# Pass over the weights in pairs of tiles through single buffers, and the square roots one GELU group earlier

## Chip, cores and metric

The kernel runs on all 8 cores of one Trainium2 chip, the same program on each with its own rows. The metric is the device time of the slowest core, in microseconds (us).

## What is computed

The input x is 4 x 8192 x 1024 in float32. It goes through a state-space layer and a quantised feed-forward layer, each behind a layer norm and added to its input:

```python
# attn: u = LN(x) @ W_in.T ; h_t = h_{t-1}*Abar + u_t*Bbar ; y = (h*C) @ W_out.T
x = x + attn(layernorm(x))
def _quant_weight(w):                       # ternary weights, one scale for the whole matrix
    s = clip(mean(abs(w)), 1e-5, None)
    return clip(round(w / s), -1, 1) * s
def _quant_act(x):                          # 8-bit activations, one scale per token
    scale = 127.0 / clip(max(abs(x), axis=-1, keepdims=True), 1e-5, None)
    return clip(round(x * scale), -128, 127) / scale
# w1: 4096 x 1024, w2: 1024 x 4096
h = gelu(quant_act(layernorm(x)) @ quant_weight(w1).T)
x = x + quant_act(h) @ quant_weight(w2).T
```

The scale of a weight matrix needs the mean of all its absolute values. So each core reads both matrices twice: pass 1 sums absolute values, pass 2 rounds to ternary and keeps the result in SBUF.

## The kernel before

Each core makes 4096 tokens of output. A program has four stages, with semaphores written out by hand on five engines.

**Set-up.** Small parameters, W_in and W_out are loaded, cast and transposed. `woctB0` and `winB` are parts of the bf16 buffer `k2`.

**Pass 1** (VectorE L427 to L446, `for j in range(NWT)`). The 64 tiles of 128 x 1024 float32 (512 KB each; 32 of w1, 32 of w2) come over three rings: tile t on ring t % 3, ring 0 issued by ScalarE, ring 1 by SyncE, ring 2 by GpSimd. Each ring has two buffers (`WSTG`) and at most one transfer in the air: `w_dma` (L151 to L162) waits until the ring's transfer before has landed, and, through `wa`, until VectorE has reduced the tile two places back in the ring. VectorE takes the tiles in order, one `tensor_reduce` each (L430). After the last one it makes the second scale (L447 to L459) with TensorE's help.

**Pass 2** (L463 to L475). The same 64 tiles over the same rings; VectorE does three operations on a tile (L470, L472, L474), TensorE transposes it (L694), ScalarE copies it to `t1T` or `t2T` (L264, L267). The first tiles of pass 2 may be fetched as soon as the ring's next-to-last tiles of pass 1 are reduced. On ScalarE the transfer of tile j stands in the same loop as the copies.

**Main loop.** Blocks of 128 tokens, 64 in all; the first 32 (NCH) run only the recurrence, so that the state is right at the second half, and the last 32 do everything. The engines run skewed: in pass b, VectorE works on the norms of blocks b+1 and b+2 and then on the maximum and rounding of block b-NCH-1, for which TensorE makes the first product (mm1) in the same pass.
TensorE's order in a pass is: `te_fa` (transposes L753, small product L763), `te_mm1` in 8 groups of 32 matmuls (L733) into two PSUM banks in turn, with the out-projection and a transpose behind group 0, then the first half of the second product `te_mm2` (32 matmuls, L789), then `te_btr` (L771, L774, L777: brings the per-token scale across partitions), then the second half of `te_mm2`. Group g of mm1 waits until GELU g-2 has emptied its bank.
ScalarE's order is: copy `xnfm` (L324), cast `hb_s`, GELUs 0 to 5 (L303), `se_sqrt2(b+1)` (L310), `se_sqrt1(b+2)` (L316), GELUs 6 and 7, copy `k1fm` (L292), `se_rowbc` (L330, L333). `sqrt2` needs VectorE's L527, `sqrt1` needs its L544, which comes later.
VectorE's order is: L592, scan L489, output L499, `ve_fb1a` (L509, L511, L514), `ve_fb1b` (L521 to L527), `ve_fa1a` (L533), `ve_fa1b` (L539 to L544), `ve_fb2` (L563 to L585, waits for `sqrt2`), `ve_fa2` (L552 to L556, waits for `sqrt1`), then `ve_back_a`: the maximum over the hidden layer (L599, waits for GELU 7), the scale (L603 to L611), and rounding in four quarters (L622, L623).

Of the kernel before, what the change touches and what calls it, by code (L numbers as in the profile page):

```python
# [6 lines left out]
F32 = mybir.dt.float32  # L7
BF16 = mybir.dt.bfloat16
AF = mybir.ActivationFunctionType
ALU = mybir.AluOpType  # L10
AX = mybir.AxisListType
# [9 lines left out]
W1_TILES = 32  # L21
W2_TILES = 32
NWT = W1_TILES + W2_TILES
# [6 lines left out]
        _PT_ORDER.append(("k", _b - NCH))  # L30
PT_IDX = {key: i for i, key in enumerate(_PT_ORDER)}

W_SLOT = []
_rc = [0, 0, 0]
for _t in range(2 * NWT):
    _r = (_t % NWT) % 3
    W_SLOT.append((_r, _rc[_r]))
    _rc[_r] += 1
W_RING = [[t for t in range(2 * NWT) if W_SLOT[t][0] == r] for r in range(3)]


def build_nc():
    nc = bass.Bass("TRN2", target_bir_lowering=False)
    dr = {}
    for n, shp in [("xh", (TOK, D)), ("xo", (TOK, D)),
# [22 lines left out]
    h_sb = sbt("h_sb", (128, H))  # L68
    vs2 = sbt("vs2", (128, 2048))
    x2 = x2_3 + [vs2[:, 1024:2048]]  # L70
    k2 = sbt("k2", (128, H), BF16)
# [19 lines left out]
    TL = {n: TLblk[:, i:i + 1] for i, n in enumerate(TLn)}  # L91
# [17 lines left out]
    wstB = [h_sb[:, 1024:2048], h_sb[:, 2048:3072]]  # L109
    wstC = [h_sb[:, 3072:4096], out_s0[:, 0:1024]]  # L110
    WSTG = [wst, wstB, wstC]
    wqb = [k2[:, 0:1024], k2[:, 1024:2048]]
    winB = k2[:, 2048:3072]
    woctB0 = k2[:, 3072:4096]
# [2 lines left out]
    wmul = x2_3[0]  # L117
    wrnd = x2_3[1]
    wabs = hred
# [8 lines left out]
    t2T_qv = t2T.rearrange("p (q f r) -> p q f r", q=4, f=8)  # L128
    pT_v8 = pT.rearrange("p (k t) -> p k t", k=8)

    SEMS = ["lx", "lw", "lws", "lwg", "lp", "lo", "gp", "prep",
            "wa", "s1b", "s2b", "q1", "q1T", "q1e",
            "zoh1", "zoh2", "k1m", "k1me", "winc", "winTd", "winTe",
            "wotc", "wotTd", "wotTe", "woctr", "wcT1", "wcT2", "sc1m", "sc2m",
# [5 lines left out]
    with ExitStack() as ctx:  # L140
# [7 lines left out]
        def wtile(j):  # L148
            return w1_v[j] if j < W1_TILES else \
                w2_v[(j - W1_TILES) // 4, (j - W1_TILES) % 4]  # L150

        def w_dma(eng, r, t):
            _, si = W_SLOT[t]
            if si >= 2:
                tp = W_RING[r][si - 2]
                if tp < NWT:
                    eng.wait_ge(S["wa"], tp + 1)
                else:
                    eng.wait_ge(S["q1"], tp - NWT + 1)
            eng.wait_ge(S[WSEM[r]], 16 * si)  # L160
            eng.dma_start(out=WSTG[r][si % 2],
                          in_=wtile(t % NWT)).then_inc(S[WSEM[r]], 16)  # L162

        @block.sync
        def _(sync):
            for di, nm in enumerate(["logA", "Bp", "Cp", "logdt", "gate", "win"]):
                dst = {"logA": P64["logA"], "Bp": P64["Bp"], "Cp": P64["Cp"],
                       "logdt": sc11, "gate": gt11}.get(nm)
                d = winF[0:64, :] if nm == "win" else dst[:]
                sync.wait_ge(S["lp"], 16 * di)  # L170
                sync.dma_start(out=d, in_=dr[nm][:, :]).then_inc(S["lp"], 16)
            wo_v = dr["wout"].rearrange("(a p) n -> a p n", p=128)
            for a in range(8):
                sync.wait_ge(S["lo"], 16 * a)
                sync.dma_start(out=wost[:, a * 64:(a + 1) * 64],
                               in_=wo_v[a]).then_inc(S["lo"], 16)
            for t in W_RING[1]:
                w_dma(sync, 1, t)
            for it in range(NIT):
                sync.wait_ge(S["lx"], 16 * it)  # L180
                if it >= 2:
                    sync.wait_ge(S["xn_"], it - 1)
                    sync.wait_ge(S["sq1a"], it - 1)
                    if it - 2 >= NCH:
                        sync.wait_ge(S["x2_"], it - 2 - NCH + 1)
                    else:
                        sync.wait_ge(S["scan"], it - 1)
                src = dr["xh"] if it < NCH else dr["xo"]
                c = it if it < NCH else it - NCH
                sync.dma_start(out=xb[it % 2][:],  # L190
                               in_=src[c * 128:(c + 1) * 128, :]).then_inc(S["lx"], 16)

        @block.gpsimd
        def _(g):
            g.iota(identD[:], pattern=[[-1, 128]], base=0, channel_multiplier=1,
                   allow_small_or_imprecise_dtypes=True)
            g.drain().then_inc(S["gp"], 1)
            for t in W_RING[2]:
                w_dma(g, 2, t)
            def gp_sq2(it):  # L200
                oi = it - NCH
                g.wait_ge(S["x2_"], oi + 1)
                if it >= NCH + 1:
                    g.wait_ge(S["k1s_"], it - NCH)
                g.tensor_tensor(scr_sq[:], x2[oi % 4][:], x2[oi % 4][:],  # L205
                                ALU.mult)
                g.drain().then_inc(S["sq2a"], 1)

            def gp_sq1(it):
                g.wait_ge(S["lx"], 16 * (it + 1))  # L210
                if it >= 1:
                    g.wait_ge(S["r1d"], it)
                if it - NCH >= 1:
                    g.wait_ge(S["r2d"], it - NCH)
                g.tensor_tensor(scr_sq[:], xb[it % 2][:], xb[it % 2][:],  # L215
                                ALU.mult)
                g.drain().then_inc(S["sq1a"], 1)

            gp_sq1(0)
            gp_sq1(1)  # L220
            for b in range(NIT + 3):
                oi3 = b - NCH - 3
                if NCH <= b + 1 < NIT:
                    gp_sq2(b + 1)
                if b + 2 < NIT:
                    gp_sq1(b + 2)
                if 0 <= oi3 < NCH:
                    g.wait_ge(S["od"], 16 * oi3)
                    g.wait_ge(S["outv"], oi3 + 1)
                    g.dma_start(out=dr["out"][oi3 * 128:(oi3 + 1) * 128, :],  # L230
                                in_=out_s[oi3 % 2][:]).then_inc(S["od"], 16)
            g.wait_ge(S["od"], 16 * NCH)

        @block.scalar
        def _(s):
# [14 lines left out]
            s.wait_ge(S["wotTd"], 1)  # L250
            s.copy(woctB0[0:64, :], pT[0:64, 0:1024])
            s.drain().then_inc(S["wotTe"], 1)
            for t in W_RING[0]:
                if t < NWT:
                    w_dma(s, 0, t)
            s.wait_ge(S["sc1m"], 2)
            s.copy(TL["r1b"][:], pmisc[:, 2:3])
            s.copy(TL["s1o"][:], pmisc[:, 3:4])
# [80 lines left out]
            for b in range(NIT + 2):  # L339
                oi1 = b - NCH - 1  # L340
                has1 = 0 <= oi1 < NCH
                if b + 1 < NIT:
                    se_xnfm(b + 1)
                if NCH <= b + 1 < NIT:
                    se_hb(b + 1)
                if has1:
                    for g in range(0, 6):
                        se_gelu(oi1, g)
                if NCH <= b + 1 < NIT:
                    se_sqrt2(b + 1)  # L350
                if b + 2 < NIT:
                    se_sqrt1(b + 2)
                if has1:
                    se_gelu(oi1, 6)
                    se_gelu(oi1, 7)
                if 0 <= b - NCH < NCH:
                    se_k1fm(b - NCH)
                if has1:
                    se_rowbc(oi1)

        @block.vector
        def _(v):
# [61 lines left out]
            v.tensor_single_scalar(woct[0:64, :], woctB0[0:64, :],  # L424
                                   P64["Cp"][:, 0:1], ALU.mult)
            D_().then_inc(S["woctr"], 1)
            for j in range(NWT):  # L427
                _r, _si = W_SLOT[j]
                v.wait_ge(S[WSEM[_r]], 16 * (_si + 1))
                v.tensor_reduce(wabs[:, j:j + 1], WSTG[_r][_si % 2], AX.X, ALU.add,  # L430
                                apply_absolute_value=True)
                D_().then_inc(S["wa"], 1)
                if j == W1_TILES - 1:
                    v.tensor_reduce(TL["wcol"][:, 0:1], wabs[:, 0:W1_TILES],
                                    AX.X, ALU.add)
                    D_().then_inc(S["wcT1"], 1)
                    v.wait_ge(S["wcT1"], 2)
                    v.tensor_reduce(wtot[0:1, 0:1], pmisc[0:1, 128:256], AX.X,
                                    ALU.add); D_()
                    v.tensor_scalar(pack[0:1, 2:3], wtot[0:1, 0:1],  # L440
                                    1.0 / (H * D), 1e-5, op0=ALU.mult,
                                    op1=ALU.max); D_()
                    v.reciprocal(pack[0:1, 0:1], pack[0:1, 2:3]); D_()
                    v.tensor_scalar(pack[0:1, 1:2], pack[0:1, 2:3],
                                    1.0 / 127.0, None, op0=ALU.mult)
                    D_().then_inc(S["sc1m"], 1)  # L446
            v.wait_ge(S["s1b"], 1)  # L447
            v.tensor_reduce(TL["wcol"][:, 0:1], wabs[:, W1_TILES:NWT],
                            AX.X, ALU.add)
            D_().then_inc(S["wcT2"], 1)  # L450
            v.wait_ge(S["wcT2"], 2)
# [10 lines left out]
            for j in range(NWT):  # L462
                rb = TL["r1b"] if j < W1_TILES else TL["r2b"]  # L463
                if j == W1_TILES:
                    v.wait_ge(S["s2b"], 1)
                _r, _si = W_SLOT[NWT + j]
                v.wait_ge(S[WSEM[_r]], 16 * (_si + 1))
                if j >= 2:
                    v.wait_ge(S["q1T"], j - 1)
                v.tensor_single_scalar(wmul[:], WSTG[_r][_si % 2], rb[:, 0:1],  # L470
                                       ALU.mult); D_()
                v.tensor_scalar(wrnd[:], wmul[:], TL["C_t"][:, 0:1],  # L472
                                TL["nC_t"][:, 0:1], op0=ALU.add, op1=ALU.add); D_()
# [376 lines left out]
```

## Time and profile before

| | us |
|---|---|
| median of the runs | 2277.48 |
| lowest and highest of 2 runs | 2272.14, 2282.82 |
| the profiled execution | 2280.37 |
| its span, slowest core (core 2) | 2278.8 |
| spans of the 8 cores | 2260.1 to 2278.8 |

The span runs from the first to the last instruction of the slowest core; the execution's own time is 1.6 us more. All shares and rows are of core 2. A line L12 is line 12 of the kernel before. DVE is VectorE, ACT ScalarE, PE TensorE, POOL GpSimd, SP SyncE. "Idle before" is the time an engine stood still ahead of an instruction, with what ended it.

### The profile page before, as it was taken

How to read it: one execution, taken by the hardware profiler on the slowest of the kernel's cores; microseconds unless marked ns; L12 is line 12 of the kernel's file. 1: busy time of each engine (PE TensorE's matmuls, PEld its weight loads, DVE VectorE, ACT ScalarE, POOL GpSimd, SP SyncE). 2: the span in 40 equal slices, each digit the busy share in tenths (PEclk: the TensorE clock that was granted, in tenths of full speed). 3: DMA queues.
4: the chain of work that ended last, by engine and by line, in shares of the span. 5: the costliest groups of instructions: out<-in, count | busy, mean ns of one | idle time of the engine just before them, and what ended most of it. 6: DMA issues, size and time to landing. Idle time of an engine off the chain costs nothing.

```text
span 2278.8 us, 34173 instructions; the slowest of 8 cores (2260.1 to 2278.8 us)
## 1 busy us (share of the span) xinstructions
PE 1225.5 (54%) x12248; PEld 852.5 (37%) x12248; DVE 1485.8 (65%) x2187; ACT 444.0 (19%) x682; POOL 223.1 (10%) x175
## 2 busy tenths in 40 slices
PE   0002222211111126777867776786778678777887
PEld 0001111111111115445644554564455456445554
DVE  3565555555555557777777777777777777777653
ACT  0002222211110112212321221222122122212210
POOL 0000000011111111000100100010010001001000
PEclk9999999999999997979988998998899889889989
DMA  4874344111111100000100000010000001000000
GB/s 138 251 247 140 118 138 157 41 42 47 46 46 46 46 19 20 19 20 20 38 19 20 29 29 19 20 38 20 19 29 29 19 19 39 20 19 20 19 11 28
DMA packets 33900, 120.18 MB, mean 53 GB/s; under 512 B 4996, under 2 KB 4996, under 8 KB 33732
## 3 DMA queue, kind: packets, MB, share of 16 engines
q1 hardware_dynamic: 16740, 56.11, 7.6%
q0 software_dynamic: 10656, 38.80, 4.5%
q10 hardware_dynamic: 6336, 23.07, 3.4%
q8 instruction: 100, 1.64, 0.3%
q14 instruction: 68, 0.56, 0.1%
HBM read 101.19 MB, written 16.78 MB: 52 GB/s over the span
## 4 chain that ended last, share of the span: by engine, by line
PE 37%; DVE 34%; DMA 10%; issue 8%; ACT 7%; DVEq 2%; ACTq 1%; POOLq 0%; SPq 0%; POOL 0%
PE pout L789 13%; DVE hred L599 10%; PE pm1b L733 8%; PE pm1a L733 8%; DMA vs<-w 5%; ACT xnfm L324 3%; DMA h_sb<-w 2%; PE pmisc L763 2%; DVE xn L556 2%; PE pT L753 2%; DVE TLblk L553 2%; DVE TLblk L539 2%; DMA out_s<-w 2%; DVE vs L533 2%; DVE TLblk L572 2%
## 5 line engine op out<-in xcount | busy, mean ns | idle before, releaser
L789 PE MATMUL pout<-t2T,k 128*128 128x512 bf16 x2048 | 507.7, 411 | 4.1 <-DVEq L504 4.1
L789 PEld LDWEIGHTS pout<-t2T,k 128*128 128x128 bf16 x2048 | 210.1, 105 | 279.6 <-issue 84.4
L733 PE MATMUL pm1a<-k1fm,t1T 128*128 128x128 bf16 x4096 | 253.7, 221 | 0.0
L733 PE MATMUL pm1b<-k1fm,t1T 128*128 128x128 bf16 x4096 | 251.3, 220 | 0.0
L622 DVE TENSOR_TENSOR vs<-h_sb,sc2bc 128x1024 f32<-128x1024 f32 x128 | 156.8, 1225 | 134.9 <-ACTq L334 75.2
L599 DVE TENSOR_REDUCE hred<-h_sb 128x128 f32<-128x4096 f32 x32 | 224.1, 7004 | 28.6 <-ACTq L305 22.8
L733 PEld LDWEIGHTS pm1a<-k1fm,t1T 128*128 128x128 bf16 x4096 | 236.7, 99 | 3.4 <-issue 0.3
L733 PEld LDWEIGHTS pm1b<-k1fm,t1T 128*128 128x128 bf16 x4096 | 235.7, 98 | 0.0
L753 PE MATMUL pT<-identb,xn 128*128 128x128 bf16 x512 | 53.5, 268 | 295.2 <-DVEq L558 295.2
L694 PE MATMUL pT<-identb,k 128*128 128x128 bf16 x512 | 64.7, 306 | 190.5 <-DVEq L476 190.5
L753 PEld LDWEIGHTS pT<-identb,xn 128*128 128x128 bf16 x512 | 42.7, 120 | 310.1 <-issue 303.5
L215 POOL TENSOR_TENSOR xn<-xb 128x1024 f32<-128x1024 f32 x64 | 121.1, 1892 | 379.9 <-DMA xb<-xh 291.4
L324 ACT COPY xnfm<-pT 128x1024 bf16<-128x1024 bf16 x64 | 64.8, 1012 | 402.9 <-PE pT L753 402.7
L771 PE MATMUL pmisc<-ident,hred 128*128 128x128 f32 x32 | 14.0, 437 | 219.2 <-DVEq L601 219.2
L205 POOL TENSOR_TENSOR xn<-x 128x1024 f32<-128x1024 f32 x24 | 45.2, 1884 | 858.7 <-DVEq L513 858.7
L694 PEld LDWEIGHTS pT<-identb,k 128*128 128x128 bf16 x512 | 49.5, 137 | 205.5 <-issue 205.5
L592 DVE TENSOR_SCALAR u_s<-pmisc,P64blk 64x128 f32<-64x128 f32 x64 | 21.9, 343 | 145.6 <-PE pmisc L763 145.3
L623 DVE TENSOR_SCALAR k<-vs,TLblk 128x1024 bf16<-128x1024 f32 x128 | 104.0, 813 | 10.8 <-issue 0.9
L763 PE MATMUL pmisc<-xnfm,winT 128*64 128x128 bf16 x512 | 54.2, 270 | 98.0 <-ACTq L325 98.0
L303 ACT ACTIVATE h_sb<-pm1b 128x512 f32<-128x512 f32 x128 | 76.4, 597 | 154.4 <-PE pm1b L733 149.8
L303 ACT ACTIVATE h_sb<-pm1a 128x512 f32<-128x512 f32 x128 | 76.4, 597 | 115.9 <-PE pm1a L733 93.0
L771 PEld LDWEIGHTS pmisc<-ident,hred 128*128 128x128 f32 x32 | 5.8, 180 | 233.8 <-issue 233.8
(152 smaller groups left out, 1444.7 us busy)
## 6 DMA issues: line engine op xcount, KB each, us to landing
vs<-w ACTq DMA_DIRECT2D x44, 512.0 KB, 4.8
h_sb<-w SPq DMA_DIRECT2D x42, 512.0 KB, 4.7
xb<-xh SPq DMA_DIRECT2D x32, 512.0 KB, 3.4
xb<-xo SPq DMA_DIRECT2D x32, 512.0 KB, 3.5
out<-out_s POOLq DMA_DIRECT2D x32, 512.0 KB, 3.0
h_sb<-w POOLq DMA_DIRECT2D x21, 512.0 KB, 5.3
out_s<-w POOLq DMA_DIRECT2D x21, 512.0 KB, 4.9
xn<-win SPq DMA_DIRECT2D x1, 256.0 KB
```

The costliest lines, as they stand in the source:

```text
L215: g.tensor_tensor(scr_sq[:], xb[it % 2][:], xb[it % 2][:], ALU.mult)
L303: s.activation(h_sb[:, g * 512:(g + 1) * 512], bank[:], AF.Gelu, bias=0.0, scale=1.0)
L324: s.copy(xnfm[it % 2][:], pT[:])
L533: v.tensor_scalar(vs2[:, 0:1024], xb[it % 2][:], 0.0, None, op0=ALU.add, op1=ALU.add, accum_out=TL["sm"][:, 0:1]); D_()
L599: v.tensor_reduce(hred[:, 0:128], h3, AX.X, ALU.max, apply_absolute_value=True)
L622: v.tensor_tensor(vq, hs, bcb, ALU.mult); D_()
L623: v.tensor_scalar(k2[:, q * 1024:(q + 1) * 1024], vs2[:, 0:1024], TL["C_t"][:, 0:1], TL["nC_t"][:, 0:1], op0=ALU.add, op1=ALU.add); D_()
L694: ti = t.transpose(pT[:, f * 128:(f + 1) * 128], wqb[j % 2][:, f * 128:(f + 1) * 128], identb[:])
L733: ti = t.matmul(reg, t1T[:, k * 4096 + m * 128:k * 4096 + (m + 1) * 128], k1fm[oi % 2][:, k * 128:(k + 1) * 128], start=(k == 0), stop=(k ...
L753: ti = t.transpose(pT[:, f * 128:(f + 1) * 128], xn[:, f * 128:(f + 1) * 128], identb[:])
L763: ti = t.matmul(pmisc[0:64, 0:128], winT[:, k * 64:(k + 1) * 64], xnfm[it % 2][:, k * 128:(k + 1) * 128], start=(k == 0), stop=(k == 7))
L789: ti = t.matmul(pout[:, d * 512:(d + 1) * 512], k2[:, hk * 128:(hk + 1) * 128], t2T[:, hk * 1024 + d * 512:hk * 1024 + d * 512 + 512], sta ...
```

## The change

It has two parts.

1. In pass 1 two neighbouring tiles are one pair: 32 pairs of 1 MB, each loaded by one DMA (a 128 x 2 x 1024 pattern for w1, 2048 neighbouring columns for w2) and reduced by one `tensor_reduce` over 2048 columns. Each ring has one buffer of 2048 columns in place of two of 1024 (`WPAIR`), so a ring's next transfer waits until its last pair is reduced. Ring 2's buffer is the whole of `k2`, so its first transfer waits for `woctr`. Pass 2 has the tiles, rings and buffers it had, but the first two transfers of every ring wait until the whole of pass 1 is reduced.
2. In the main loop ScalarE does GELUs 0 to 4, then the two square roots, then GELUs 5 to 7.

```diff
+P1_RING = [[p for p in range(NP1) if p % 3 == r] for r in range(3)]
...
+    k2f = k2.bitcast(F32)
+    WPAIR = [vs2[:, 0:2048], h_sb[:, 1024:3072], k2f[:, 0:2048]]
...
+        def w_dma1(eng, r, i):
+            p = P1_RING[r][i]
+            if i >= 1:
+                pprev = P1_RING[r][i - 1]
+                eng.wait_ge(S["wa"], pprev + 1)
+            if r == 2 and i == 0:
+                eng.wait_ge(S["woctr"], 1)
+            eng.wait_ge(S[WSEM[r]], 16 * i)
+            eng.dma_start(out=WPAIR[r].rearrange("p (c d) -> p c d", c=2),
+                          in_=wpairsrc(p)).then_inc(S[WSEM[r]], 16)
...
         def w_dma(eng, r, t):
-            if si >= 2:
-                tp = W_RING[r][si - 2]
-                if tp < NWT:
-                    eng.wait_ge(S["wa"], tp + 1)
-                else:
-                    eng.wait_ge(S["q1"], tp - NWT + 1)
+            if i2 < 2:
+                eng.wait_ge(S["wa"], NP1)
+            else:
+                tp = P2_RING[r][i2 - 2]
+                eng.wait_ge(S["q1"], tp + 1)
...
                 if has1:
-                    for g in range(0, 6):
+                    for g in range(0, 5):
                         se_gelu(oi1, g)
                 if NCH <= b + 1 < NIT:
                     se_sqrt2(b + 1)
                 if b + 2 < NIT:
                     se_sqrt1(b + 2)
                 if has1:
-                    se_gelu(oi1, 6)
-                    se_gelu(oi1, 7)
+                    for g in range(5, 8):
+                        se_gelu(oi1, g)
...
-            for j in range(NWT):
-                _r, _si = W_SLOT[j]
+            for p in range(NP1):
+                _r, _si = P1_SLOT[p]
                 v.wait_ge(S[WSEM[_r]], 16 * (_si + 1))
-                v.tensor_reduce(wabs[:, j:j + 1], WSTG[_r][_si % 2], AX.X, ALU.add,
+                v.tensor_reduce(wabs[:, p:p + 1], WPAIR[_r], AX.X, ALU.add,
                                 apply_absolute_value=True)
```

## Rows read from the trace of the kernel before

**Rows 1.** Busy time of the engines in three stages, and each stage's granted clock.

```profile
core 2: us, PE busy (x) PEld busy (x) DVE busy (x) ACT busy (x) POOL busy (x), PEclk, DMA share, GB/s
34.00:166.00 132.00, 0.93 (x3) 0.57 (x3) 79.17 (x71) 0.22 (x2) 10.55 (x20) 1.00 0.82 253
166.00:422.00 256.00, 64.65 (x507) 49.32 (x507) 145.15 (x197) 63.98 (x65) 12.64 (x21) 1.00 0.39 130
...
885.00:2210.00 1325.00, 1007.93 (x10452) 694.50 (x10451) 971.78 (x1367) 313.19 (x503) 124.79 (x86) 0.88 0.07 23
```

**Rows 2.** Waits from 38 to 158 us: waiter, releaser, us in total, times, longest.

```profile
POOL out_s L161 <- DMA h_sb<-w: 51.1, 8, 7.3
POOL h_sb L161 <- DMA out_s<-w: 42.5, 8, 5.8
SPq L157 <- DVEq L432: 104.4, 20, 8.6
```

**Rows 3.** Median time from issue to landing, whole page, section on DMA issues.

```profile
vs<-w ACTq DMA_DIRECT2D x44, 512.0 KB, 4.8
xb<-xh SPq DMA_DIRECT2D x32, 512.0 KB, 3.4
```

**Rows 4.** Timeline of pass 1 and its end: start, duration, instruction, [idle before].

```profile
33.66 36.62 ACTq L161 DMA_DIRECT2D vs<-w  x8
...
45.64 1.22 DVE L430 TENSOR_REDUCE hred<-out_s 128x1 f32<-128x1024 f32 x1 [0.19 <-issue]
...
164.52 1.22 DVE L430 TENSOR_REDUCE hred<-vs 128x1 f32<-128x1024 f32 x1 [0.19 <-issue]
...
168.05 0.75 DVE L470 TENSOR_SCALAR x<-vs,TLblk 128x1024 f32<-128x1024 f32 x1 [0.33 <-issue]
...
169.77 0.69 DVE L474 TENSOR_SCALAR k<-x 128x1024 bf16<-128x1024 f32 x1
```

**Rows 5.** Timeline of one pass of the main loop, around the square roots.

```profile
1534.58 1.28 ACT L310 ACT_TABLE_LOAD   x1
1535.37 1.95 PE L733 MATMUL pm1b<-k1fm,t1T 128*128 128x128 bf16 x32
1535.38 0.15 DVE L544 TENSOR_SCALAR TLblk<-TLblk 128x1 f32<-128x1 f32 x1
1535.87 0.20 ACT L310 ACTIVATE TLblk<-TLblk 128x1 f32<-128x1 f32 x1
1536.20 0.16 DVE L563 RECIPROCAL TLblk<-TLblk 128x1 f32<-128x1 f32 x1 [0.67 <-ACTq L312]
...
1537.16 7.07 PE L789 MATMUL pout<-t2T,k 128*128 128x512 bf16 x32
1537.87 0.60 ACT L303 ACTIVATE h_sb<-pm1a 128x512 f32<-128x512 f32 x1
...
1543.89 6.99 DVE L599 TENSOR_REDUCE hred<-h_sb 128x128 f32<-128x4096 f32 x1 [0.19 <-issue]
1551.17 0.45 PE L771 MATMUL pmisc<-ident,hred 128*128 128x128 f32 x1 [6.95 <-DVEq L601]
...
1554.78 8.78 PE L789 MATMUL pout<-t2T,k 128*128 128x512 bf16 x32
```

**Rows 6.** The line L563 over the whole span: idle of VectorE before it.

```profile
  ACTq L312: 26.9, 30
```

**Rows 7.** TensorE alone in short stretches: busy time (matmuls), granted clock, DMA.

```profile
1019.75:1025.77 6.02, 6.02 (x16) 0.50 0.00 0
1025.77:1028.50 2.73, 2.73 (x14) 1.00 0.00 0
1065.68:1070.15 4.47, 4.47 (x12) 0.50 0.00 0
1244.07:1247.64 3.57, 3.57 (x10) 0.50 0.00 0
1288.44:1292.01 3.57, 3.57 (x10) 0.50 0.00 0
1510.47:1513.88 3.41, 3.41 (x10) 0.50 0.00 0
1548.00:1554.78 6.78, 1.51 (x4) 0.50 0.00 0
1554.78:1558.25 3.47, 3.47 (x10) 0.50 0.00 0
1558.25:1563.55 5.30, 5.30 (x28) 1.00 0.00 0
```

More of the change, by code:

```diff
@@ L31 @@
 PT_IDX = {key: i for i, key in enumerate(_PT_ORDER)}
[L33 to L39, printed above, removed]
+NP1 = NWT // 2
+P1_RING = [[p for p in range(NP1) if p % 3 == r] for r in range(3)]
+P1_SLOT = {}
+for _r in range(3):
+    for _i, _p in enumerate(P1_RING[_r]):
+        P1_SLOT[_p] = (_r, _i)
+P2_RING = [[j for j in range(NWT) if j % 3 == r] for r in range(3)]
+P2_SLOT = {}
+for _r in range(3):
+    for _i, _j in enumerate(P2_RING[_r]):
+        P2_SLOT[_j] = (_r, len(P1_RING[_r]) + _i)
 def build_nc():
@@ L129, in build_nc @@
     pT_v8 = pT.rearrange("p (k t) -> p k t", k=8)
-    SEMS = ["lx", "lw", "lws", "lwg", "lp", "lo", "gp", "prep",
+    SEMS = ["lx", "lw", "lws", "lwg", "lwt", "lp", "lo", "gp", "prep",
             "wa", "s1b", "s2b", "q1", "q1T", "q1e",
@@ L150, in wtile, with wpairsrc @@
                 w2_v[(j - W1_TILES) // 4, (j - W1_TILES) % 4]
-        def w_dma(eng, r, t):
-            _, si = W_SLOT[t]
-            if si >= 2:
-                tp = W_RING[r][si - 2]
-                if tp < NWT:
-                    eng.wait_ge(S["wa"], tp + 1)
-                else:
-                    eng.wait_ge(S["q1"], tp - NWT + 1)
+        w1_pv = dr["w1"].rearrange("(a c p) d -> a p c d", c=2, p=128)
+        w2_pv = dr["w2"].rearrange("(i p) (b e) -> i b p e", p=128, e=2048)
+        def wpairsrc(p):
+            if p < W1_TILES // 2:
+                return w1_pv[p]
+            pp = p - W1_TILES // 2
+            return w2_pv[pp // 2, pp % 2].rearrange("p (c d) -> p c d", c=2)
+        def w_dma1(eng, r, i):
[8 more added lines that the diff above has]
+                          in_=wpairsrc(p)).then_inc(S[WSEM[r]], 16)
+        def w_dma(eng, r, t):
+            j = t - NWT
+            _, si = P2_SLOT[j]
+            i2 = si - len(P1_RING[r])
+            if i2 < 2:
[3 more added lines that the diff above has]
+                eng.wait_ge(S["q1"], tp + 1)
             eng.wait_ge(S[WSEM[r]], 16 * si)
-            eng.dma_start(out=WSTG[r][si % 2],
-                          in_=wtile(t % NWT)).then_inc(S[WSEM[r]], 16)
+            eng.dma_start(out=WSTG[r][i2 % 2],
+                          in_=wtile(j)).then_inc(S[WSEM[r]], 16)
         @block.sync
@@ L176, in _ @@
                                in_=wo_v[a]).then_inc(S["lo"], 16)
-            for t in W_RING[1]:
-                w_dma(sync, 1, t)
+            for i in range(len(P1_RING[1])):
+                w_dma1(sync, 1, i)
+            for j in P2_RING[1]:
+                w_dma(sync, 1, NWT + j)
             for it in range(NIT):
@@ L197, in _ @@
             g.drain().then_inc(S["gp"], 1)
-            for t in W_RING[2]:
-                w_dma(g, 2, t)
+            for i in range(len(P1_RING[2])):
+                w_dma1(g, 2, i)
+            for j in P2_RING[2]:
+                w_dma(g, 2, NWT + j)
             def gp_sq2(it):
@@ L252, in _ @@
             s.drain().then_inc(S["wotTe"], 1)
-            for t in W_RING[0]:
-                if t < NWT:
-                    w_dma(s, 0, t)
+            for i in range(len(P1_RING[0])):
+                w_dma1(s, 0, i)
             s.wait_ge(S["sc1m"], 2)
@@ L426, in _ @@
             D_().then_inc(S["woctr"], 1)
-            for j in range(NWT):
-                _r, _si = W_SLOT[j]
+            for p in range(NP1):
+                _r, _si = P1_SLOT[p]
                 v.wait_ge(S[WSEM[_r]], 16 * (_si + 1))
-                v.tensor_reduce(wabs[:, j:j + 1], WSTG[_r][_si % 2], AX.X, ALU.add,
+                v.tensor_reduce(wabs[:, p:p + 1], WPAIR[_r], AX.X, ALU.add,
                                 apply_absolute_value=True)
                 D_().then_inc(S["wa"], 1)
-                if j == W1_TILES - 1:
-                    v.tensor_reduce(TL["wcol"][:, 0:1], wabs[:, 0:W1_TILES],
+                if p == NP1 // 2 - 1:
+                    v.tensor_reduce(TL["wcol"][:, 0:1], wabs[:, 0:NP1 // 2],
                                     AX.X, ALU.add)
@@ L447, in _ @@
             v.wait_ge(S["s1b"], 1)
-            v.tensor_reduce(TL["wcol"][:, 0:1], wabs[:, W1_TILES:NWT],
+            v.tensor_reduce(TL["wcol"][:, 0:1], wabs[:, NP1 // 2:NP1],
                             AX.X, ALU.add)
@@ L465, in _ @@
                     v.wait_ge(S["s2b"], 1)
-                _r, _si = W_SLOT[NWT + j]
+                _r, _si = P2_SLOT[j]
+                _i2 = _si - len(P1_RING[_r])
                 v.wait_ge(S[WSEM[_r]], 16 * (_si + 1))
@@ L469, in _ @@
                     v.wait_ge(S["q1T"], j - 1)
-                v.tensor_single_scalar(wmul[:], WSTG[_r][_si % 2], rb[:, 0:1],
+                v.tensor_single_scalar(wmul[:], WSTG[_r][_i2 % 2], rb[:, 0:1],
                                        ALU.mult); D_()
```

## The prediction

> **What bounds the kernel now.** I cut the span into stages first, because the two parts of the change live in different ones [rows 1]. Pass 1 (34 to 166 us) is 6% of the span, pass 2 11%, and the main loop with everything in it (885 to 2210 us) 58%. In pass 1 TensorE and ScalarE are idle, VectorE is busy 60%, and the DMA engines 82%: it is bound by transfers.
>
> The waits say how. GpSimd's ring waits 93.6 us in 16 waits for its own last landing, 5.85 us each [rows 2]. With its issue of some 0.55 us this ring turns every 6.4 us and never stops. SyncE's ring has time left: it waits 104.4 us for VectorE, which takes tiles in order and so goes at the pace of the slowest ring. The pace from the sixth reduce (45.64) to the 64th (164.52) is 118.9 us for 58 tiles, 2.05 each, 12.3 for six [rows 4].
>
> In the main loop no engine is full (TensorE 76%, VectorE 73%), so I followed one pass in the timeline [rows 5]. VectorE has L544 done at 1535.53 but starts L563 only at 1536.20, because ScalarE's `sqrt2` is queued behind GELU 5 and a table load of 1.28 us. Over the whole run that idle time is 26.9 us in 30 waits [rows 6], with some long ones at the start; the usual one is 0.67 or a little less. From L563 on VectorE runs without a gap to L599, then TensorE's L771, then the second half of mm2 at 1554.78, which leads to the next pass.
>
> The clock is the third thing to see [rows 7]. TensorE has done nothing since 1544.2 when the clock falls from 2.4 to 1.2 GHz at 1548.0, and it rises at 1558.25, after 3.47 us of matmuls of the second half. That half takes 8.78 us, the first 7.07 at full clock: the difference, 1.71, is half of 3.47. So a low stretch of s us under matmuls costs s/2.
>
> Now set the rises beside the starts. The second half starts at 1019.75, 1065.68, 1244.07, 1288.44, 1510.47 and 1554.78; the clock rises at 1025.77, 1070.15, 1247.64, 1292.01, 1513.88 and 1558.25. Between the first and the last rise lie 12 passes and 532.48 us, 44.373 a pass, and the neighbouring pairs give 44.38, 44.37 and 44.37. The starts don't keep this step: 45.93, 44.37, 44.31. The low stretch makes up the difference: pass length less s/2 is 45.93 - 3.01 = 42.92, 44.37 - 1.79 = 42.58, 44.31 - 1.71 = 42.60. A pass whose work is about 42.6 us is held at 44.37: if it starts its second half early, the rise doesn't come early with it, s grows, and half of what was gained is paid at once. The rest is paid in the passes behind (s: 6.02, 4.47, ... 3.57, 3.57). This is the choice on which my forecast of the loop rests.
>
> **Part 1, pass 1.** Removed: 32 of 64 transfers and reduces. The 2048-column reduce has no row; it lies between 1.22 (the cost of 1024) and 2.44 (twice that), and nearer the latter, since an instruction over one column still takes 0.15 (L544 [rows 5]): 2 x (1.22 - 0.15) + 0.15 = 2.3. VectorE then needs 32 x 2.5 = 80 us of 130, so it is no bound, but now it stands in the ring: a cycle of a ring is landing + 2.3 + about 0.2 + issue 0.55, for 1 MB. Per ring before: 12.3 us for 1 MB.
> The landing of 1 MB has no row either. At least: 5.85 and another 512 KB at the whole measured rate of 253 GB/s (2.1), so 7.9 and a cycle of 10.9; then three rings move 3.15 MB in 10.9, 289 GB/s. At most: two landings of 512 KB, 11.7, cycle 14.7. If the second 512 KB gets half the rate (4.1), it is 13.0. Fewer transfers are in the air while a ring waits for its reduce, so the others go faster; I take 12.0, between 10.9 and 13.0, which is 262 GB/s and near the measured rate. Start: ring 0 issues at 33.66 as before and the first pair lands at about 40; pairs 1 (early, on SyncE) and 2 (issued after `woctr`, at 34.2) follow, so three pairs are reduced at about 47, as six tiles are now (45.64 + 1.22). Left are 29 pairs, 9.67 cycles: 9.67 x (12.0 - 12.3) = -2.9. The last reduce is 1.1 longer.
> Hand-over to pass 2: now VectorE ends pass 1 at 165.74 and starts L470 at 168.05, 2.3 us, the tile long there. After it, all three rings wait for the last `wa`; a landing takes 4.8 on ScalarE's ring [rows 3], plus 0.1: +2.6. Queued behind these waits are only later weight transfers; ScalarE has its scale copy done by then (before `w_dma` of tile 64 in its order). Pass 2 itself is unchanged, so it is moved and not stretched. Sum of part 1: -2.9 + 1.1 + 2.6 = +0.8; bounds 9.67 x (10.9 - 12.3) + 3.7 = -10 and 9.67 x (14.7 - 12.3) + 3.7 = +27.
> The Trainium skill (DMA: Bandwidth & Descriptors, Anatomy of one DMA) fits a transfer as about 2.0 us and its bytes at 436 GB/s; by that 1 MB costs 2 us less than two of 512 KB, an estimate of 19 us less for pass 1. The landing of 5.85 us for 512 KB, where that fit has 3.2, shows that the eight cores are not in that regime. Against the change speaks the rule to double-buffer (Trainium Kernel Development and Optimization, Best Practices).
>
> **Part 2, the main loop.** `sqrt2` now stands behind GELU 4, whose input is one group (1.8 us) earlier, and is done before L544 ends. L563 then starts 0.19 behind L544, as other instructions do that wait for nothing [rows 5]: 0.67 - 0.19 = 0.48 less, say 0.45. Nothing below zero is to be had from VectorE.
> What ScalarE does later: `sqrt1` can't start before 1535.53 + 0.1; with 0.20 for itself and 1.4 for the table load GELU 5 starts at 1537.2 and ends at 1537.8, where it ended at 1534.4, just ahead of the table load. Group 7 of mm1 waits for that bank: 1537.95 in place of 1535.37, end 1539.9 (1541.9 at the low clock), GELU 7 at the latest at 1542.6. L599 starts at 1543.4, so it is covered by 0.8 to 2.8 us. The first half of mm2 ends at about 1547.0, and L771 is due at 1550.7: covered by 3.7. Queued behind are the `k1fm` copy and the row copies, not due before 1553. TensorE stands idle 2.5 us before group 7, and the clock may fall there; that is hidden as long as these covers last. The number of table loads is unchanged.
> So the work of a pass falls from 42.6 to 42.15. By the lock, s goes from 3.5 to 4.4, within the 6.02 that rows 7 show, and the pass stays at 44.37. Over the loop only the earlier phase at its end is kept, about -1.
>
> **Sum** against the profiled 2280.4: +0.8 - 1 = 2280.2; the median of the runs is 2.9 lower. I say **2277**.
>
> **Rivals.**
> A (forecast): held loop, pass 1 within 10 us: 2277, its own range 2267 to 2290. 0.62.
> B: larger transfers pay. Cycle of 10.9 or less: -10 to -20 us, 2262. For it: DMA share 0.82, not 1; against: landings of 5.85 under load. 0.12.
> C: the lock gives way. 28 passes x 0.45 = 13 us, 2264; if the low stretch under the second half vanishes also, 28 x (0.45 + 1.71) = 60 us, 2217. For it: with the first half of mm2 ending at 1547.0 and L771 at 1550.7, TensorE's idle time falls from 6.9 to about 4 us, and the clock might stay up. The Trainium skill (TensorE: Matmul & The Clock Gate, HAM oscillation) has short gaps leave the clock alone. Against the large one: TensorE also has only 1.5 us of work from 1548.0 to 1554.8, and the clock didn't rise in it. 0.14 for the small gain, 0.05 for the large.
> D, slower: one buffer a ring costs pass 1 its overlap. With landings of 1 MB at 11.7 the cycle is 14.7: +27 us, 2303; it is slower as soon as the landing exceeds 9.3. For it: 104.4 us of waits of SyncE's ring for VectorE, which now every ring has. Against: TensorE and ScalarE's idle, and freed rate. 0.05.
> E, slower by more: the clock falls in the gap before group 7 and stays low. Low for all of group 7 and the first half of mm2, they end at 1556.0, L771 is 5.3 us late, 28 x 5.3 = +148 us, 2425. It decides from a low stretch of 7.4 us on (twice the 3.7 of cover). Rows 7 show low stretches under matmuls of 3.4 to 6.0 us. 0.02.
>
> **Numbers.** A range from 2248 to 2296 leaves out the large C, E and the ends of B and D. A measurement of this kernel tells about 2% from no change. Below 2232 only the large C: 0.05. Above 2323: E, 0.02. Within: 0.93.
>
> **What would show it.** Pass 1: 32 reduces of 2.3 us ending near 166, at 250 to 270 GB/s. Hand-over of 5 us before the first L470. Main loop: idle before L563 near 0.2, a new idle time of about 2.5 us of TensorE before group 7, with a dip of the clock there; passes still 44.37 apart with s of about 4.4. Wrong if the passes are 43.9 or less apart, if L599 waits for GELU 7, or if pass 1 is more than 10 us off.

## The result, and the profile after

The changed kernel takes 2256.51 us (median of 11 runs, 2249.18 to 2264.93) against 2279.46 for the kernel before in the same comparison (10 runs). The ratio is 0.9897 with a 95% interval of 0.988 to 0.9914: 23 us, 1.0%, less. The forecast was 2277 with a range of 2248 to 2296. The profiled execution of the changed kernel has a slowest core (core 0) of 2261.1 us; the cores lie between 2238.3 and 2261.1.

Where the 23 us went is read at six marks in both traces, as the median over the eight cores, in us:

| mark | before | after | difference |
|---|---|---|---|
| last reduce of pass 1 ends | 163.6 | 145.0 | -18.6 |
| pass 2 starts | 165.9 | 150.8 | -15.1 |
| pass 2 ends | 415.9 | 398.9 | -17.0 |
| first maximum of the main loop (before L599, after L630) | 867.6 | 849.8 | -17.8 |
| last maximum | 2225.8 | 2201.6 | -24.2 |
| end of the span | 2270.7 | 2249.1 | -21.6 |

So the start of the main loop is some 18 us earlier, by pass 1, and its end with what follows gives some 4 us more. This is one execution of each kernel; how far others with the same code differ is said below. The stages of the changed kernel (stretch, busy us and count of each engine, granted clock, DMA share, GB/s), to be set against [rows 1]:

```profile
core 0: us, PE busy (x) PEld busy (x) DVE busy (x) ACT busy (x) POOL busy (x), PEclk, DMA share, GB/s
34.00:146.00 112.00, 1.30 (x4) 0.66 (x4) 74.70 (x41) 0.32 (x2) 6.08 (x10) 1.00 0.92 288
150.00:411.00 261.00, 63.73 (x504) 48.77 (x504) 144.01 (x192) 63.98 (x65) 12.98 (x21) 1.00 0.39 127
```

Pass 1 moves 288 GB/s in place of 253. The timeline of its third pair, its last pair and the first operation of pass 2:

```profile
42.21 2.29 DVE L460 TENSOR_REDUCE hred<-k 128x1 f32<-128x2048 f32 x1 [0.19 <-issue]
...
142.03 2.29 DVE L460 TENSOR_REDUCE hred<-h_sb 128x1 f32<-128x2048 f32 x1 [0.57 <-DMA h_sb<-w]
...
149.58 0.75 DVE L501 TENSOR_SCALAR x<-vs,TLblk 128x1024 f32<-128x1024 f32 x1 [2.91 <-DMA vs<-w]
```

A reduce over 2048 columns takes 2.29, as estimated. From the third pair (end 44.50) to the 32nd (144.32) are 99.8 us for 29 pairs, 10.3 for three, where six tiles took 12.3 [rows 4]. The hand-over takes 5.3 us, and in the last 2.91 of it VectorE has nothing left to wait for but the landing. Landings in the middle of the pass:

```profile
k<-w POOLq DMA_DIRECT2D x9, 1024.0 KB, 7.4
vs<-w ACTq DMA_DIRECT2D x9, 1024.0 KB, 8.1
```

and who waited for whom from 42 to 138 us (compare [rows 2]): GpSimd's ring no longer runs from landing to landing, it waits for the reduce of its pair.

```profile
POOL k L175 <- DVEq L462: 88.9, 9, 11.4
```

One pass of the main loop of the changed kernel, lines as in [rows 5]:

```profile
1515.06 1.28 ACT L340 ACT_TABLE_LOAD   x1
...
1516.35 0.20 ACT L340 ACTIVATE TLblk<-TLblk 128x1 f32<-128x1 f32 x1
...
1517.67 0.15 DVE L575 TENSOR_SCALAR TLblk<-TLblk 128x1 f32<-128x1 f32 x1
...
1518.02 0.16 DVE L594 RECIPROCAL TLblk<-TLblk 128x1 f32<-128x1 f32 x1 [0.19 <-issue]
...
1520.35 3.48 PE L764 MATMUL pm1b<-k1fm,t1T 128*128 128x128 bf16 x32 [2.55 <-ACTq L335]
...
1523.93 0.60 ACT L333 ACTIVATE h_sb<-pm1b 128x512 f32<-128x512 f32 x1 [2.99 <-PE pm1b L764]
...
1525.71 7.11 DVE L630 TENSOR_REDUCE hred<-h_sb 128x128 f32<-128x4096 f32 x1 [0.19 <-issue]
1533.11 0.30 PE L802 MATMUL pmisc<-ident,hred 128*128 128x128 f32 x1 [2.28 <-DVEq L632]
```

The square root is done at 1516.55, and the reciprocal of the second norm (L594) starts 0.20 behind the end of L575, in place of 0.67; over the run VectorE's idle time before it is 5.7 us in 29 short stops and 5.2 in three waits for ScalarE, where it was 26.9 in 30 [rows 6]:

```profile
  issue: 5.7, 29
  ACTq L342: 5.2, 3
```

TensorE waits 2.55 us before group 7 of mm1 (2.5 forecast) and then takes 3.48 for it in place of 1.95, at the low clock. GELU 7 ends at 1524.53, 1.2 us before the maximum starts: the cover, put at 0.8 to 2.8, held. TensorE's idle time before the transpose of the maxima is 2.28, down from 6.95. Now the clock (TensorE alone: busy time and matmuls, granted clock, DMA), as in [rows 7]:

```profile
1359.55:1363.47 3.92, 3.92 (x11) 0.50 0.00 0
1448.31:1452.21 3.90, 3.90 (x11) 0.50 0.00 2
1520.50:1523.88 3.38, 3.33 (x32) 0.50 0.02 5
1530.85:1534.10 3.25, 0.30 (x1) 1.00 0.00 0
1534.13:1536.57 2.44, 1.06 (x3) 0.50 0.00 0
1536.57:1540.96 4.39, 4.39 (x12) 0.50 0.00 0
1540.96:1545.70 4.74, 4.69 (x24) 1.00 0.00 0
```

The rises at 1363.47, 1452.21 and 1540.96 are 88.74 and 88.75 apart, two passes of 44.37 each. The second half of mm2 starts 3.9 to 4.4 us before them, where it was 3.4 to 3.6 [rows 7]. Over 20 passes in the middle of the loop and all eight cores the median of this stretch is 4.3, where it was 3.4. The row 1520.50 is the new dip at group 7. It was hidden, since TensorE still waits 2.28 us for the maxima behind it. The clock is low for as long as before: from 1548.01 to 1558.25 then, 10.2 us in one piece [rows 7], and now 3.4 us at group 7 and 6.8 from 1534.13 to 1540.96.

### The profile page after: what moved, and what is told of

Its sections match the earlier page's. It is cut to its first block, busy times and chain, and to the rows that moved or that the text cites. A ratio compares the mean times of both kernels' runs of the same rounds, so it can differ in the third digit from the quotient of the medians.

```text
span 2261.1 us, 33922 instructions; the slowest of 8 cores (2238.3 to 2261.1 us)
## 1 busy us (share of the span) xinstructions
PE 1274.6 (56%) x12185; PEld 893.2 (40%) x12248; DVE 1483.0 (66%) x2155; ACT 444.1 (20%) x682; POOL 218.7 (10%) x164
## 4 chain that ended last, share of the span: by engine, by line
DVE 46%; PE 24%; issue 9%; DMA 9%; ACT 5%; DVEq 4%; POOLq 3%; ACTq 0%; POOL 0%; SPq 0%
PE pout L820 13%; DVE hred L630 10%; DMA vs<-w 6%; DVE TLblk L570 3%; DVE vs L564 3%; ACT xnfm L354 3%; POOLq L238 3%; PE pmisc L794 2%; DVE xn L587 2%; DVE TLblk L556 2%; PE pT L784 2%; DVE TLblk L584 2%; DVE TLblk L603 2%; DMA h_sb<-w 2%; DVE TLblk L552 2%
## 5 line engine op out<-in xcount | busy, mean ns | idle before, releaser
L764 PE MATMUL pm1b<-k1fm,t1T 128*128 128x128 bf16 x4096 | 290.2, 237 | 73.0 <-ACTq L335 73.0
L764 PEld LDWEIGHTS pm1b<-k1fm,t1T 128*128 128x128 bf16 x4096 | 272.2, 108 | 77.3 <-issue 77.3
L630 DVE TENSOR_REDUCE hred<-h_sb 128x128 f32<-128x4096 f32 x32 | 227.2, 7099 | 28.2 <-ACTq L335 22.4
L564 DVE TENSOR_SCALAR_CACHE_REDUCE vs<-xb 128x1024 f32<-128x1024 f32 x64 | 78.1, 1220 | 13.5 <-issue 13.1
L794 PEld LDWEIGHTS pmisc<-xnfm,winT 128*64 128x64 bf16 x512 | 42.8, 142 | 110.4 <-issue 110.4
```

What stands on the lines that cost most here:

```text
L564: v.tensor_scalar(vs2[:, 0:1024], xb[it % 2][:], 0.0, None, op0=ALU.add, op1=ALU.add, accum_out=TL["sm"][:, 0:1]); D_()
L630: v.tensor_reduce(hred[:, 0:128], h3, AX.X, ALU.max, apply_absolute_value=True)
L764: ti = t.matmul(reg, t1T[:, k * 4096 + m * 128:k * 4096 + (m + 1) * 128], k1fm[oi % 2][:, k * 128:(k + 1) * 128], start=(k == 0), stop=(k ...
L794: ti = t.matmul(pmisc[0:64, 0:128], winT[:, k * 64:(k + 1) * 64], xnfm[it % 2][:, k * 128:(k + 1) * 128], start=(k == 0), stop=(k == 7))
```

## Experiments

Each was compared with the kernel before on its own chip, so the ratios are to be compared and not the medians. Lengths of passes are the mean distance of the starts of the maximum, over 25 passes in the middle of the loop, median over the cores. The pace of pass 1 is the time from the sixth tile's (third pair's) reduce to the last, for 3 MB, worked out from the marks in the same way.

### The two parts apart, and the clock taken out of the loop

`p1_only` is the changed kernel with this undone:

```diff
-                    for g in range(0, 5):
+                    for g in range(0, 6):
                         se_gelu(oi1, g)
...
-                    for g in range(5, 8):
-                        se_gelu(oi1, g)
+                    se_gelu(oi1, 6)
+                    se_gelu(oi1, 7)
```

> The changed kernel with the square roots back behind GELU 5; only pass 1 and its hand-over are changed against the kernel before. If the gain of the change sits in pass 1 (last reduce 18.6 us earlier, median of cores, hand-over 3.5 us longer) and the main loop is held at 44.37 us a pass by the clock, the time is 16 to 20 us under the kernel before (ratio 0.991 to 0.993) and the passes of the loop keep 44.37 with a low stretch of about 3.4 us under the second half of mm2. If the square roots carry part of it (rival, 28 x 0.45 = 13 us), only some 10 us are left (ratio 0.996).

`sq_only` is the kernel before with the opposite edit.

> The kernel before with the square roots one GELU earlier, pass 1 as before. Held loop: 1 to 5 us under the kernel before (ratio 0.998 to 1.000), idle before the reciprocal of the second norm 0.2 us in place of 0.67, passes 44.37 apart, low stretch under the second half about 4.4 us. Rival, loop not held: 28 x 0.45 = 13 us less, ratio 0.994, passes 43.9 apart.

`warm_before` and `warm_after` put matmuls into TensorE's waits. They write into `pssm`, whose content has been used by then, and nothing reads them:

```diff
+            def fill(n):
+                for _ in range(n):
+                    t.matmul(pssm[:, 0:512], identb[:], t2T[:, 0:512],
+                             start=True, stop=True)
...
                     te_mm2(oi2, range(0, 16))
+                if has1 and has2 and w_it is not None:
+                    t.wait_ge(S["x2_"], w_it - NCH + 1)
+                    fill(28)
```

with `fill(5)` ahead of the wait for `sc2_` and `fill(1)` ahead of the wait for `rowe` in `te_btr`. `warm_after` has `fill(14)` in place of `fill(28)`, and `fill(9)` before group 7 of mm1.

> The kernel before with extra matmuls of constant operands that fill TensorE's idle time in a full pass: 28 of 128x512 between the first half of mm2 and the transpose of the maxima, 5 and 1 in the two short waits behind it. Nothing waits for their results. If the clock holds the loop, the fall of the clock goes away, and a pass takes its work of 42.6 us: 28 x 1.77 = 50 us less, 2229, ratio 0.978. If a pass is held at 44.37 by anything else, the time stays within 5 us of the kernel before.

> The changed kernel with the same kind of filling (9 matmuls before group 7 of mm1, 14 behind the first half of mm2, 5 and 1 behind that). With the clock up, the 0.45 us that the earlier square roots save show in the pass: 42.15 us a pass, 28 x 2.22 = 62 us under the changed kernel, about 2195, ratio to the kernel before 0.963; 13 us more than the same filling gives the kernel before, beside what pass 1 gives. If the earlier square roots save nothing even then, passes are 42.6.

| kernel | median, us | ratio to before (95%) | a pass, us |
|---|---|---|---|
| before | 2279.46 | | 44.41 |
| changed | 2256.51 | 0.9897 (0.988 to 0.9914) | 44.39 |
| p1_only | 2260.96 | 0.9897 (0.9878 to 0.9916) | 44.40 |
| sq_only | 2280.42 | 0.9983 (0.9963 to 1.0003) | 44.36 |
| warm_before | 2242.19 | 0.9835 (0.9789 to 0.9881) | 42.37 |
| warm_after | 2199.61 | 0.9632 (0.961 to 0.9654) | 41.91 |

The four kernels with and without the earlier square roots have the same pass of 44.4 while the clock falls in every pass; 28 x 0.45 = 13 us of saved work bring nothing there that `sq_only` can tell from zero.

`p1_only` gained 23 us, more than the 16 to 20 expected, and has the ratio of the changed kernel, which has 4 us of the loop besides. That fits with how much pass 1 differs from one execution to another. In the four kernels with the pass 1 of the change (the changed one, `p1_only`, `warm_after`, `p2_ahead`) it ends at 145.0, 146.3, 147.3 and 149.5; in those with the old pass 1 at 163.6 (before), 170.0 (`sq_only`) and 170.6 (`warm_before`). `p1_only` and `sq_only`, on one chip, are 23.7 us apart there. So pass 1 gives 18.6 in the profiled pair and some 14 to 26 over all of these, and the times alone can't divide the gain. The loop's share is read inside a trace: from the first maximum to the last, `sq_only` takes 6.9 us less than the kernel before (1358.2 to 1351.3), and behind the last 2.6 more, so the earlier square roots give some 4 us.

With the waits filled the clock stays up. This is TensorE alone from 1200 to 2000 us, first in `warm_before`:

```profile
1200.00:2000.00 800.00, 733.39 (x7277) 1.00 0.08 26
```

then in `warm_after`:

```profile
1200.00:2000.00 800.00, 724.13 (x7221) 1.00 0.08 26
```

and a pass takes 42.37 and 41.91. The difference of 0.46 is the idle time that the earlier square roots remove: before L563 VectorE still waits 26.6 us for ScalarE in 30 times in `warm_before`, and the filling is not in the way, as TensorE has 1.04 us left to wait behind it. So the saved work was real in the changed kernel, and the clock took it. In `warm_after` the second half of mm2 takes 7.08 (1507.42) where the kernel before needs 8.78 [rows 5]; the 14 filling matmuls in front of the transpose (L804) leave 0.91 of idle time:

```profile
1500.27 3.19 PE L804 MATMUL pssm<-t2T,identb 128*128 128x512 bf16 x14
1504.37 0.30 PE L811 MATMUL pmisc<-ident,hred 128*128 128x128 f32 x1 [0.91 <-DVEq L632]
1504.50 1.24 PE L804 MATMUL pssm<-t2T,identb 128*128 128x512 bf16 x5
1506.25 0.27 PE L816 MATMUL pmisc<-ident,TLblk 128*1 128x128 f32 x1 [0.50 <-DVEq L644]
...
1507.42 7.08 PE L833 MATMUL pout<-t2T,k 128*128 128x512 bf16 x32
```

The transposes are quicker too (L811 takes 0.30, where L771 takes 0.45 at the low clock), which may be why a pass falls 0.2 below the 42.6 of the forecast. `warm_before` gained 42 us where 50 were expected. Its loop from the first to the last maximum did fall by 58.8 us (1358.2 to 1299.4). But the passes with the recurrence alone, in which nothing was changed, take 11.82 in the filled kernels against 11.62 to 11.64 in the others, 6 us in all, and pass 2 of `warm_before` takes 253.1 in place of 250.0. Both stay unexplained, and the interval of its ratio, 0.979 to 0.988, leaves anything between 27 and 48 us open.

### What makes pass 1 faster

`single_512k` is the kernel before with one buffer a ring: pass 1 loads every tile of ring r into `WSTG[r][0]`, after this wait.

```diff
-            if si >= 2:
-                tp = W_RING[r][si - 2]
-                if tp < NWT:
-                    eng.wait_ge(S["wa"], tp + 1)
+            if t < NWT and si >= 1:
+                eng.wait_ge(S["wa"], W_RING[r][si - 1] + 1)
...
```

> The kernel before with one buffer of 512 KB a ring in pass 1 in place of two (64 transfers, 64 reduces as before; the first transfers of pass 2 wait until the ring's last tile is reduced). It takes the single buffers of the change without its larger transfers. If the size of a transfer makes the gain, this is slower than before: a ring adds 1.4 us of reduce to its cycle, 3 MB take 13 us or more in place of 12.1 (median of cores and both matrices), pass 1 ends 8 to 15 us later. Rival: if it is the spreading of the rings by the single buffers (fewer transfers in the air at once) that makes the gain, 3 MB take 11 us or less and pass 1 ends earlier.

`two_512k` is the changed kernel with two transfers for a pair, and the counts of the ring's semaphore to match:

```diff
-            eng.dma_start(out=WPAIR[r].rearrange("p (c d) -> p c d", c=2),
-                          in_=wpairsrc(p)).then_inc(S[WSEM[r]], 16)
+            for c in range(2):
+                eng.dma_start(out=WPAIR[r][:, c * 1024:(c + 1) * 1024],
+                              in_=wtile(2 * p + c)).then_inc(S[WSEM[r]], 16)
```

> The changed kernel with each pair loaded by two transfers of 512 KB that are issued back to back in the same ring. If what counts is that a ring has 1 MB in the air between two waits, the pace stays at 10.3 us for 3 MB and the time at that of the changed kernel (2256, ratio 0.990). If a transfer of 1 MB is itself moved faster, the pace falls back towards 12 us and the time to 2270 or more.

`pieces_4k` changes the pairs of w2:

```diff
-        w2_pv = dr["w2"].rearrange("(i p) (b e) -> i b p e", p=128, e=2048)
+        w2_pv = dr["w2"].rearrange("(a c p) (q d) -> a q p c d", c=2, p=128,
+                                   d=1024)
```

> The changed kernel with the pairs of w2 made of two row blocks of 1024 columns, so that w2 comes in pieces of 4 KB as w1 does, not of 8 KB. If the pieces count, the pace of w2 goes from 10.0 to 10.6 us for 3 MB (that of w1) or, if the long rows of w2 cost it as they do before, to 11.4: 3 to 8 us in all. If they don't count, the pace of w2 stays at 10.0 and the time at 2256.

`two_buffers_1m` gives each ring two buffers of 1 MB (`WPAIR[r][i % 2]`, in `t1T`):

```diff
-            if i >= 1:
-                pprev = P1_RING[r][i - 1]
+            if i >= 2:
+                pprev = P1_RING[r][i - 2]
```

> The changed kernel with two buffers of 1 MB a ring in pass 1, in the space of the transposed w1 that is not yet written; the hand-over to pass 2 is unchanged. If the wait for the ring's own reduce still costs, the cycle of a ring falls from 10.3 to about 9 us (landing 7.7, issue 0.6, some more sharing) and pass 1 ends 10 us earlier, 2246. If the transfer engines are the bound at their share of 0.91 and 302 GB/s, more in the air brings at most 3 us.

| kernel | ratio (95%) | 3rd MB-pair or 6th tile reduced | pass 1 ends | pace, us for 3 MB |
|---|---|---|---|---|
| before | | 45.6 | 163.6 | 12.2 |
| changed | 0.9897 (0.988 to 0.9914) | 45.5 | 145.0 | 10.3 |
| single_512k | 1.0053 (1.003 to 1.0075) | 49.4 | 179.8 | 13.5 |
| two_512k | 0.9894 (0.9865 to 0.9923) | 46.7 | 149.1 | 10.6 |
| pieces_4k | 0.988 (0.9851 to 0.9909) | 46.8 | 149.0 | 10.6 |
| two_buffers_1m | 0.9879 (0.9854 to 0.9904) | 53.1 | 144.8 | 9.5 |

The same code gives paces of 12.2 to 12.7 (old pass 1) and 10.3 to 10.6 (new pass 1) in the executions named above, so smaller differences than these tell nothing. The single buffers cost, as the forecast's slower rival had it: alone they make the pace 13.5, and pass 1 ends at 179.8. What pays is the other half of the change, and not because a transfer of 1 MB is moved better. Two transfers of 512 KB issued back to back do as well: 10.6, an end at 149.1 and the ratio 0.9894 can't be told from the changed kernel. What counts is how much a ring has in the air from one wait to the next. No kernel was run that keeps the 64 reduces and the two buffers and drops only the ring's wait for its last landing, so this is shown for single buffers. The landings of `single_512k` and its engines' rows from 45 to 135 us are

```profile
h_sb<-w POOLq DMA_DIRECT2D x12, 512.0 KB, 5.0
vs<-w ACTq DMA_DIRECT2D x12, 512.0 KB, 5.2
```

```profile
45.00:135.00 90.00, 0.93 (x3) 0.57 (x3) 46.97 (x43) 0.00 (x0) 6.36 (x12) 1.00 0.77 222
```

so 512 KB land in 5.0 to 5.2 and 1 MB in 7.4 to 8.1. The second 512 KB cost some 2.6 us; if the first cost as much for its bytes, another 2.5 or so, an estimate, are paid once for every wait, whatever it carries.

`pieces_4k` shows no effect of the size of the pieces: w2 goes at 10.3 for 3 MB in place of 10.0, but w1, which it leaves alone, also at 10.8 in place of 10.6.

`two_buffers_1m` falsified its expectation of 10 us; what came is the other outcome named there, at most 3 us. Pass 1 ends where it ended, though its first three pairs come 7.6 us later. One cause is likely, but wasn't tested: GpSimd's ring now loads two pairs during the set-up, and ScalarE's first transfer is issued at 38.4 where it was at 31.6 (medians). Its pace of 9.5 is no faster transfer: on the slowest core VectorE takes the first nine pairs one behind the other, since they have landed by the time it comes to them. From 45 to 135 us its slowest core moves the same as that of the changed kernel, which is shown here first for the changed one

```profile
45.00:135.00 90.00, 0.93 (x3) 0.58 (x3) 60.00 (x31) 0.32 (x2) 5.55 (x9) 1.00 0.97 304
```

and then for `two_buffers_1m`:

```profile
45.00:135.00 90.00, 0.92 (x3) 0.58 (x3) 66.33 (x34) 0.22 (x2) 4.83 (x8) 1.00 0.97 304
```

A DMA share of 0.97 and 304 GB/s: with 1 MB a ring in the air the transfers themselves have become the bound (3 MB at that rate are 10.3 us, the pace of the changed kernel), and a single buffer is enough to reach it.

### A version that beats both

The trace of the changed kernel has one more wait of this kind. In pass 2 ScalarE issues the transfer of its ring in the same loop as its copies, at the moment it is needed; VectorE's waits from 166 to 410 us are

```profile
DVE x L501 <- DMA vs<-w: 87.9, 20, 6.0
```

`p2_ahead` moves that issue three tiles forward:

```diff
-                if j % 3 == 0:
-                    w_dma(s, 0, NWT + j)
+                if j == 0:
+                    w_dma(s, 0, NWT)
+                if j % 3 == 0 and j + 3 < NWT:
+                    w_dma(s, 0, NWT + j + 3)
```

> The changed kernel with one thing more: in pass 2 ScalarE issues the transfer of tile j+3 where it issued that of tile j, so that its ring is one transfer ahead as the two other rings are. In the changed kernel VectorE waits about 4.3 us for that ring before every third tile (12.3 us for three tiles whose work is 8.0). If only that late issue stands in the way, pass 2 takes about 175 us in place of 248, the time is 70 us under the changed kernel, 2187, ratio to the kernel before 0.959. If the transfers are the bound (3 tiles in 8.0 us are 196 GB/s, pass 1 moved 304), less. The main loop stays at 44.37 a pass.

`all_four` adds the filling of `warm_after`, and pair buffers in `t1T`, so that pass 2 needn't wait for the last reduces.

> The changed kernel with the filling matmuls of the main loop, ScalarE one transfer ahead in pass 2, and the pair buffers of pass 1 moved into the space of the transposed w1, so that the first transfers of pass 2 need not wait for the last reduces. The parts lie in different stages and should add: 2200 (filling) - 70 (pass 2) - 4 (hand-over back to some 2 us) = about 2126, ratio 0.932. If one takes the other's gain, the sum falls short of 2140.

| kernel | median, us | ratio (95%) | pass 2 | hand-over | a pass |
|---|---|---|---|---|---|
| p2_ahead | 2182.85 | 0.9555 (0.9527 to 0.9583) | 173.2 | 5.9 | 44.40 |
| all_four | 2119.25 | 0.9294 (0.9258 to 0.9331) | 173.1 | 2.7 | 41.98 |

VectorE's waits for that ring in `p2_ahead`, from 155 to 330 us:

```profile
DVE x L503 <- DMA vs<-w: 2.9, 1, 2.9
```

Pass 2 goes from 248.1 to 173.2 us, and the main loop, though it starts 70 us earlier, keeps its 44.40. `all_four` takes 2119.25, 7.1% less than the kernel before, where 2126 were expected from the sum of the parts: they add.

## Why the prediction was right where it was, and wrong where it was

**The main loop: right, in mechanism and size.** The work saved was put at 0.45 a pass; the filled kernels show 0.46. The forecast that the fixed rises of the clock would swallow it held: passes of 44.39, rises 44.37 apart, the low stretch under the second half up from 3.4 to 4.3, medians (forecast from 3.5 to 4.4). What the forecast didn't have is that the low time of a pass stays 10.2 us as a whole and is split in two. The dip before group 7 came and was hidden. Rival C, the lock giving way, did not come about; its large form, 2217, took extra matmuls to get. Rival E had no part.

The gain that remained in the loop was put at 1 us and is 4, since the lock didn't hold at its two ends. The first two distances between maxima fell by 4.3 us together (44.64 and 45.79 to 42.42 and 43.73), two near the end by 2.2 (42.36 and 36.12 to 40.88 and 35.45), and behind the last maximum 2.7 were lost again, 44.8 to 47.5, since two low stretches there last longer. `sq_only` shows the same 47.4, and `p1_only`, without the earlier square roots, 44.8.

**Pass 1: wrong step, the landing of 1 MB.** That the measured 2256.5 lies in the stated range is no merit of this part. By its own sign (pass 1 more than 10 us off) it was wrong: the last reduce came 18.6 us earlier, and rival A, the forecast with its chance of 0.62, had 2267 as its lower end. The reduce of 2.29 and the start at 45.5 (47 forecast) were right. The hand-over cost 3.5 more, where 2.6 were counted. The 1.1 for the longer last reduce was counted twice: the cycles ran from the end of one reduce to the end of another and held it already. But the pace was put at 12.0 and its lower bound at 10.9, and it is 10.3. The error is in the term "landing": 7.9 at least, taken as nearly 9, and measured as 7.4 to 8.1. I took the 5.85 us of a 512 KB landing as if all of it had to be paid before the next 512 KB began. It holds a part that doesn't grow with the bytes, which is now paid half as often, and a part that the rings made by being in each other's way: with single buffers the same 512 KB landed in 5.0 to 5.2. And the 253 GB/s that I called the whole rate were a mean over a stretch with a DMA share of 0.82; with the share at 0.97 it is 304. So the range reached its low side by rival B, whose time of 2262 is the nearest to the measured one, and which had been given 0.12. Its condition, a cycle of 10.9 or less, is what happened. The sum of part 1 was put at +0.8 and is -15.1 at the start of pass 2: 9.67 x (10.3 - 12.2) = -18.4 and +3.5 for the hand-over give -14.9.

The Trainium skill (DMA: Bandwidth & Descriptors, Anatomy of one DMA) gives a transfer a constant part of about 2.0 us and a part by its bytes, in a fit for transfers that GpSimd issues. The trace agrees in the form: the part paid per wait is about 2.5 us, an estimate from landings of 5.1 and 7.4 to 8.1. It differs in the rate of the rest: the slowest core moves 304 GB/s and not 436. The estimate of 19 us less for pass 1, which the prediction worked out from that fit, comes near the 18.6 measured by luck. It leaves out what the single buffers cost; from `single_512k` to the changed kernel, where the buffers are single in both, 3 MB take 3.2 us less (13.5 to 10.3), where the fit has 2. The same page of the Trainium skill advises transfers of 1 MB and more (Rules for kernel authors); `two_512k` shows that two of 512 KB without a wait between them bring the same here.

**Rival D** was right in its cause, since one buffer a ring costs about 1 us for 3 MB at 512 KB (13.5 against 12.2 to 12.7), and wrong in the size of the landing, 7.4 to 8.1 against the 9.3 from which it would have decided.

## What to carry to other kernels

Before counting what a loop gains from less work, set the rises of the clock beside the passes. Where they keep one step while the starts move, as here, saved work can go into slow matmuls; in this kernel it was freed by keeping TensorE busy through its waits. And before dividing a gain of 1% among the parts of a change, see how far executions of the same code differ in each stage: here 4 to 7 us in pass 1 alone. For a loop of transfers with a wait each, ask how many bytes are in the air from one wait to the next, and price the landing in two parts, one for each wait and one for the bytes. A transfer that is issued from a queue with work of its own should be issued a turn early.

## What was not expected of the hardware

TensorE's clock held the loop at 44.37 a pass for two amounts of work that differ by 0.45 us, and its falling and rising cost 2.0 to 2.5 us a pass in all (44.41 to 42.37, 44.39 to 41.91); 29 matmuls of no use in the waits of a pass took the changed kernel from a ratio of 0.990 to 0.963. The clock was low for 10.2 us in every pass of the middle of the loop, in both kernels, in one piece before and in two after. The recurrence passes, unchanged, take 0.2 us longer in the filled kernels, and no run says why.
